# Router of a mixture of experts: rows transposed in place, plain float32 products with rows stationary

## The chip, the cores and the metric

One core of one Trainium2 chip runs the whole program in one launch. The metric is the device time of one execution in microseconds (us). TensorE is called PE here (its weight loads PEld), VectorE DVE, ScalarE ACT, GpSimd POOL, SyncE SP.

## The reference, cut to what matters

The model has two layers; the change touches the router at the head of the last part. 4096 tokens (4 x 1024) of width 256 come out of a windowed attention with a residual and a layer norm, and go through a layer of 8 experts:

```python
x = _layernorm(x + _L1_attn_ref(x, ...), axis=-1)          # ends the stage before
# _L1_ffn_ref
xt = x.reshape(T, H)                                        # T = 4096, H = 256
scores = jax.nn.softmax(xt @ Wr, axis=-1)                   # Wr: 256 x 8, float32
topk_w, topk_idx = jax.lax.top_k(scores, TOP_K)             # 2 of 8 experts
topk_w = topk_w / (topk_w.sum(axis=-1, keepdims=True) + EPS)
# every token's two experts, silu(x Wg) * (x Wu) @ Wd, weighted; plus a shared expert on all tokens
```

## The kernel before, in words

X holds the tokens in SBUF as 32 tiles of 128 rows x 256 columns; four tiles are a chunk, and there are NCH = 8 chunks. The engines run programs of their own, in the order in which the code writes them, and meet by semaphores. Three stages matter:

- **The attention's tail.** The loop over chunks on PE, `step(c, h)`, makes scores, transposes the exponentials (`p_transpose`, L1795) and makes outputs. DVE adds the residual and takes the statistics, POOL makes the inverse deviation, and ACT normalises the chunk in place in X (`normalise_chunk`, L554, semaphore `c_ln`). With chunk 7 this ends the stage.
- **The router**, which starts when `c_ln` says that all 8 chunks are normalised. For each chunk DVE copies the rows to `dxc` (L1354), PE transposes the 8 blocks of 128 x 128 (`x_transpose`, L1857) into PSUM, ACT rounds the result to `DTh` (L608), and DVE takes the rest to `DTl` (L1358), both in the float32r format. PE then makes the logits of 512 tokens with the router's weights stationary (8 columns) and the rows moving (512 columns), as three products of high and low parts for each half of the width (`three`, L1577 to L1579): 6 matmuls. They come out as 8 x 512, by expert; ACT copies them to `lgT` (L618), PE turns them by four small transposes (`by_token`, L1875), and DVE copies them to `lg` (L1362).
- **The routing and what hangs on it.** DVE alone takes the softmax, the two best experts, the counts and each token's place (L1394 to L1468), with one exponential on ACT and two matmuls on PE between. Its last instruction writes `pos` and raises `d_route`. Then POOL scatters the tokens by 64 indirect DMAs (L869), while PE, ACT and DVE work the shared expert for the first four chunks (`shared`). When both are through, the tiles of the experts begin (L1551 and on), then the shared expert for the other four chunks, the gathers and the last layer norm.

PE's `x_transpose(NCH, ...)` and DVE's `copy_rows(NCH + ...)` repeat the transposes of the same chunks for the shared expert, since `DTh` and `DTl` hold two chunks only.

The router's step on PE and the start of the routing on DVE:

```python
            def route(c, h):
                x_transpose(c + 1, 1 - h, 4 - 4 * h)
                router(c, h)
...
            dve.tensor_reduce(rt[0][:], lg[:], AX.X, ALU.max)
            dve.drain()
            dve.tensor_tensor(lg[:], lg[:], each(rt[0][:]), ALU.subtract).then_inc(d_max, 1)
```

Of the kernel before, what the change touches and what calls it, by code (L numbers as in the profile page):

```python
# [4 lines left out]
F32 = mybir.dt.float32  # L5
F32R = mybir.dt.float32r
BF16 = mybir.dt.bfloat16
U32, U16 = mybir.dt.uint32, mybir.dt.uint16
ALU = mybir.AluOpType
# [66 lines left out]
def build(nc, cst, xT, x, wqkvgT, wave_cols, bias_cols, coupling_rows, woutT, bout, wgu_rows, wd_rows, wqk_T, wo_rows, bo, wr, experts, out):  # L76
    ctx = ExitStack()
    with ctx:
        place = {"at": 0, "top": 0}

        def sb(name, shape, dt=F32):
            size = 2 if dt == BF16 else 4
            for s in shape[1:]:
                size *= s
            t = nc.alloc_sbuf_tensor_at(name, shape, dt, offset=base + place["at"])
            place["at"] += (size + 31) // 32 * 32
            place["top"] = max(place["top"], place["at"])
            return t

        def sem(name):  # L90
# [91 lines left out]
        place["at"] = kept + TOP  # L182
        place["at"] += 4 * 2 * 4 * D
        cw = sb("cw", [P, 3, KD, D])
# [22 lines left out]
        wrr = sb("wrr", [P, KD, E])  # L207
        wrh, wrl = sb("wrh", [P, KD, E], F32R), sb("wrl", [P, KD, E], F32R)
        pos = sb("pos", [P, 2, NT], mybir.dt.int32)
# [28 lines left out]
        past = sb("past", [P, NE + 1])  # L238
        lgT = sb("lgT", [E, 2, CH])
        assert place["at"] <= slot_at + 4 * SLOT  # L240
# [10 lines left out]
        rstd4, nmr4 = sb("rstd4", [P, NCH, 4]), sb("nmr4", [P, NCH, 4])  # L251
        d_sum, d_cnt, d_lt, d_lth = sem("d_sum"), sem("d_cnt"), sem("d_lt"), sem("d_lth")
        (d_ld, d_xc, d_xt, d_xhi, d_xlo, d_lg, d_lgc, d_max, d_exp, d_oh, d_pre, d_route, d_sc, d_raw, d_shi, d_slo, d_gu, d_si,
         d_hb, d_hhi, d_hlo, d_dn, d_add, d_xe0, d_xe1, e_t, e_xhi, e_xlo, e_gu, e_si, e_hb, e_ht, e_hhi, e_hlo, e_dn, e_y,
         e_st0, e_st1, w_ready, d_mv, d_rs, d_ln) = (sem("d_" + n) for n in (
            "ld", "xc", "xt", "xhi", "xlo", "lg", "lgc", "max", "exp", "oh", "pre", "route", "sc", "raw", "shi", "slo", "gu", "si",
            "hb", "hhi", "hlo", "dn", "add", "xe0", "xe1", "et", "exhi", "exlo", "egu", "esi", "ehb", "eht", "ehhi", "ehlo",
# [80 lines left out]
        def _(act):  # L338
# [234 lines left out]
            normalise(NP - 1, 1)  # L573

            def step_chunk(c, h):
                if live(c, 0, NCH):
                    exponentials(c, 0)
                if live(c, -2, NCH - 2):
                    x_high(c + 2, h)
                if live(c, 0, NCH):  # L580
                    exponentials(c, 1)
                if live(c, -1, NCH - 1):
                    y_high(c + 1, 1 - h)
                if live(c, 0, NCH):
                    p_high(c)
                if live(c, -1, NCH - 1):
                    z_high(c + 1, 1 - h)
                if live(c, 1, NCH + 1):
                    normalise_chunk(c - 1, 1 - h)
# [8 lines left out]
            act.activation(SWh[:], raw[:, 1], ACT.Copy).then_inc(d_shi, 1)  # L598
            act.wait_ge(d_ld, 16)
            act.activation(wrh[:], wrr[:], ACT.Copy).then_inc(d_shi, 1)  # L600
            for c in range(NCH - 2, NCH + 1):
                step_chunk(c, c % 2)


# [4 lines left out]

            def routed(c, h):  # L610

                wait(act, d_lt, c - 1)
                x_high(c, h, 4 * h)

            def logits(c, h):
                act.wait_ge(d_lt, c + 1)
                wait(act, d_lg, c - 1)
                act.activation(lgT[:, h], PS[0:E, 2 + h], ACT.Copy).then_inc(d_lth, 1)  # L618

            routed(0, 0)  # L620
            routed(1, 1)
            logits(0, 0)
            with act.Fori(1, B) as b:
                for h in range(2):
                    routed(2 * b + h, h)
                    logits(2 * b + h - 1, 1 - h)
            logits(NCH - 1, 1)
            act.wait_ge(d_max, 1)
# [3 lines left out]
            def shared(c, h, after=True):  # L632
# [8 lines left out]
                if after:  # L641
                    x_high(NCH + c + 1, 1 - h, 0)

# [27 lines left out]

            x_high(NCH, 0, 0)
            shared(0, 0)
# [239 lines left out]
        def _(dve):  # L913
# [426 lines left out]
            with dve.Fori(1, B - 1) as b:  # L1340
                for h in range(2):
                    step(2 * b + h, h)
            dve.wait_ge(d_shi, 2)
            dve.tensor_tensor(SWl[:], raw[:, 1], SWh[:].bitcast(F32), ALU.subtract).then_inc(d_slo, 1)
            dve.tensor_tensor(wrl[:], wrr[:], wrh[:].bitcast(F32), ALU.subtract).then_inc(d_slo, 1)
            for c in range(NCH - 2, NCH + 1):
# [12 lines left out]

            def logits(c, h):  # L1360
                dve.wait_ge(d_lg, c + 1)
                dve.tensor_copy(lg[:, bass.ds(4 * c, 4)], PS[:, 6 + h, 0:4 * E].rearrange("p (w e) -> p w e", e=E)).then_inc(d_lgc, 1)  # L1362


            dve.wait_ge(c_ln, NCH)
            copy_rows(0, 0, 0)
            copy_rows(1, 1, 1)
            x_low(0, 0, 0)
            copy_rows(2, 2, 0)
            x_low(1, 1, 4)  # L1370
            with dve.Fori(0, B - 2) as b:
                for h in range(2):
                    c = 2 * b + h
                    copy_rows(c + 3, c + 3, 1 - h)
                    x_low(c + 2, h, 4 * h)
                    logits(c, h)
            copy_rows(NCH - 1, NCH - 1, 1)
            x_low(NCH - 2, 0, 0)
            logits(NCH - 4, 0)
            copy_rows(NCH, 0, 0)  # L1380
            x_low(NCH - 1, 1, 4)
            logits(NCH - 3, 1)
            copy_rows(NCH + 1, 1, 1)
            logits(NCH - 2, 0)
            logits(NCH - 1, 1)
            dve.drain()

# [9 lines left out]

            dve.tensor_reduce(rt[0][:], lg[:], AX.X, ALU.max)
            dve.drain()
            dve.tensor_tensor(lg[:], lg[:], each(rt[0][:]), ALU.subtract).then_inc(d_max, 1)  # L1400
            dve.wait_ge(d_exp, 1)
# [87 lines left out]
            def shared(c, h, early, after=True, done=()):  # L1489
# [8 lines left out]
                if after:  # L1498
                    x_low(NCH + c + 1, 1 - h, 0)
                    if not isinstance(c, int) or c + 2 < NCH:  # L1500
                        copy_rows(NCH + c + 2, c + 2, h)
                for d in done:
# [40 lines left out]

            x_low(NCH, 0, 0)
            shared(0, 0, True)
            shared(1, 1, True)
            with dve.Fori(1, EARLY // 2) as b:
                for h in range(2):
                    shared(2 * b + h, h, True)
            dve.wait_ge(d_shi, 3)  # L1550
            dve.tensor_tensor(EWs[:, EW:SLOT], raw[:, 0], EWs[:, 0:EW].bitcast(F32), ALU.subtract).then_inc(w_ready, 1)  # L1551
# [22 lines left out]
        def _(pe):  # L1574
# [269 lines left out]
            values(0, 0)  # L1844
            for c in range(NCH):
                step(c, c % 2)


            pe.wait_ge(c_res, 4 * NCH)

# [8 lines left out]

            def router(c, h):  # L1860
                pe.wait_ge(d_xlo, c + 1)

                wait(pe, d_lth, c)
                wait(pe, d_lgc, c - 2)
                for k in range(KD):
                    mm = three(PS[0:E, 2 + h], wrh[:, k], wrl[:, k], DTh[:, h, k], DTl[:, h, k], k == 0, k == KD - 1)
                mm.then_inc(d_lt, 1)

            def by_token(c, h):

                if isinstance(c, int) and c == NCH - 1:
                    pe.wait_ge(d_lth, NCH)
                    pe.wait_ge(d_lgc, NCH - 2)
                for w in range(4):
                    t = pe.transpose(PS[:, 6 + h, w * E:(w + 1) * E], lgT[:, h, w * P:(w + 1) * P], ident[0:E, 0:E])  # L1875
                t.then_inc(d_lg, 1)

            def route(c, h):
                x_transpose(c + 1, 1 - h, 4 - 4 * h)
                router(c, h)  # L1880

            pe.wait_ge(d_slo, 2)
            x_transpose(0, 0, 0)
            route(0, 0)
            route(1, 1)
            by_token(0, 0)
            with pe.Fori(1, B - 1) as b:
                for h in range(2):
                    route(2 * b + h, h)
                    by_token(2 * b + h - 1, 1 - h)  # L1890
            route(NCH - 2, 0)
            by_token(NCH - 3, 1)
            router(NCH - 1, 1)
            by_token(NCH - 2, 0)
            by_token(NCH - 1, 1)

            pe.wait_ge(d_oh, 1)
            pe.matmul(PS[:, 4, 0:NT * E], tri[:], ohr[:], start=True, stop=True).then_inc(d_pre, 1)
            pe.matmul(PS[:, 5, 0:NT * E], ones[:], ohr[:], start=True, stop=True).then_inc(d_pre, 1)
            x_transpose(NCH, 0, 0)  # L1900

            def shared(c, h, after=True):
                pe.wait_ge(d_xlo, c + NCH + 1)
                for j in range(4):
# [9 lines left out]
                if after:  # L1914
                    x_transpose(NCH + c + 1, 1 - h, 0)
                for w in range(4):
# [159 lines left out]
```

## Time and profile before

| | |
|---|---|
| median of 3 runs | 1211.71 us (1211.48 to 1213.06) |
| the profiled execution, its own time | 1211.7 us |
| its span, first to last instruction | 1209.9 us |
| PE busy | 1039.7 us (86%) |
| DVE busy | 805.6 us (67%) |
| ACT busy, POOL busy | 467.9 us (39%), 446.5 us (37%) |
| mean granted TensorE clock | 0.939 of full speed |

The profile gives each instruction's start and duration. A matmul's duration holds its latency, so a row of matmuls overlaps and its pace is read from the distance between starts. "Granted clock" is the share of full speed (2.4 GHz) that TensorE was given: 1.00 or 0.50 at any one time, and a mean between them over a stretch.

### The profile page before, as it was taken

What the parts mean: (1) busy time and instruction counts of PE and PEld (TensorE: products, weight loads), DVE (VectorE), ACT (ScalarE), POOL (GpSimd) and SP (SyncE); (2) the same over time, 40 slices, a digit from 0 to 9 for tenths busy, and PEclk for the clock granted to TensorE, in tenths of its full rate; (3) what the DMA queues carried; (4) which work ended last, traced back from release to release, by engine and by line L of the source; (5) the groups of instructions that cost most, each with busy time, mean ns of one, the idle gap of its engine ahead of it and who ended that gap; (6) DMA issues with size and microseconds to landing.
All of it is one profiled execution on the core that took longest, in us unless ns stands there. A gap on an engine that the chain in (4) does not pass through costs nothing.

```text
span 1209.9 us, 19337 instructions
## 1 busy us (share of the span) xinstructions
PE 1039.7 (86%) x5928; PEld 907.7 (75%) x5929; DVE 805.6 (67%) x1361; ACT 467.9 (39%) x799; POOL 446.5 (37%) x357
## 2 busy tenths in 40 slices
PE   4789972589999999998675987999999999998872
PEld 3567741589999998997644876888888888887762
DVE  7978898799999986787566344444444444443775
ACT  6726523244444435565442132332223323322225
POOL 3302003134444456231104777244413431005764
PEclk9989986799999999999787898999999999999896
DMA  6110020900000000200001221333223131112324
GB/s 272 36 35 1 1 78 1 337 3 1 0 0 0 0 2 1 106 1 34 20 1 52 101 101 57 105 104 108 70 86 104 52 108 53 52 48 75 102 81 170
DMA packets 42387, 77.30 MB, mean 64 GB/s; under 512 B 5474, under 2 KB 32868, under 8 KB 40932
## 3 DMA queue, kind: packets, MB, share of 16 engines
q1 hardware_dynamic: 24532, 40.52, 9.3%
q0 software_dynamic: 7008, 26.22, 6.6%
q10 hardware_dynamic: 10800, 9.94, 2.7%
q8 instruction: 28, 0.46, 0.2%
q14 instruction: 19, 0.16, 0.0%
HBM read 45.47 MB, written 31.20 MB: 63 GB/s over the span
## 4 chain that ended last, share of the span: by engine, by line
PE 61%; DVE 13%; issue 9%; DVEq 6%; POOL 6%; ACT 3%; POOLq 1%; DMA 1%; ACTq 0%
PE PS L1577 16%; PE PS L1579 15%; PE PS L1578 15%; POOL gathered L886 5%; PE PS L1701 4%; PE PS L1947 3%; PE PS L1606 2%; DVEq L1101 1%; PE PS L1931 1%; PE PS L1619 1%; DVEq L1206 1%; DVEq L1114 1%; ACT X L703 1%; PE PS L1694 1%; DVEq L1218 1%
## 5 line engine op out<-in xcount | busy, mean ns | idle before, releaser
L1521 DVE TENSOR_TENSOR hb<-PS,gs 128x512 f32<-128x512 f32 x71 | 49.1, 692 | 153.2 <-ACT gs L652 153.2
L1577 PE MATMUL PS<-EWs,xeh 128*128 x284 | 119.2, 420 | 2.2 <-DVE xel L1515 2.2
L1579 PE MATMUL PS<-EWs,xel 128*128 x284 | 112.3, 395 | 0.0
L1578 PE MATMUL PS<-EWs,xeh 128*128 x284 | 111.9, 394 | 0.0
L886 POOL DMA_INDIRECT gathered<-expert_outputs,pos x64 | 63.1, 986 | 115.3 <-DMA expert_outputs<-ye 96.0
L1577 PE MATMUL PS<-WGh,bxh 128*128 128x352 f32 x256 | 87.2, 341 | 20.5 <-DVE hv L1200 14.3
L652 ACT ACTIVATE gs<-PS 128x512 f32<-128x512 f32 x71 | 42.5, 599 | 160.5 <-PE PS L1579 160.5
L860 POOL TENSOR_TENSOR EWs<-raw,zrow 128x3072 fp32r<-128x3072 f32 x7 | 47.7, 6816 | 149.8 <-PE PS L1579 149.7
L1701 PE MATMUL PS<-WD,htf 128*128 128x256 f32 x384 | 88.5, 380 | 1.6 <-ACT htf L470 1.5
L869 POOL DMA_INDIRECT tokens_by_expert<-X,pos x64 | 64.6, 1009 | 67.8 <-DVE pos L1468 48.5
L1577 PE MATMUL PS<-EWs,heh 128*128 x284 | 85.9, 303 | 1.6 <-DVE hel L1525 1.6
L1578 PE MATMUL PS<-WGl,bxh 128*128 128x352 f32 x256 | 84.3, 329 | 0.0
L1579 PE MATMUL PS<-WGh,bxl 128*128 128x352 f32 x256 | 84.3, 329 | 0.0
L1525 DVE TENSOR_TENSOR hel<-PS,heh 128x512 fp32r<-128x512 f32 x71 | 49.1, 692 | 47.8 <-ACT heh L657 47.8
L1578 PE MATMUL PS<-EWs,heh 128*128 x284 | 80.1, 282 | 0.0
L1579 PE MATMUL PS<-EWs,hel 128*128 x284 | 80.1, 282 | 0.0
L1701 PEld LDWEIGHTS PS<-WD,htf 128*128 128x128 f32 x384 | 71.2, 190 | 10.9 <-ACT htf L470 2.5
L657 ACT ACTIVATE heh<-PS 128x512 fp32r<-128x512 f32 x71 | 42.5, 599 | 91.1 <-PE PS L1947 91.1
L1577 PE MATMUL PS<-xh,WQh 128*128 128x512 f32 x128 | 52.8, 413 | 20.8 <-DVE WQl L936 13.4
L1577 PEld LDWEIGHTS PS<-WGh,bxh 128*128 128x128 f32 x256 | 49.6, 194 | 24.3 <-issue 15.5
L1577 PEld LDWEIGHTS PS<-EWs,xeh 128*128 128x128 f32 x284 | 53.7, 189 | 14.5 <-issue 2.4
L1577 PE MATMUL PS<-SWh,Hh 128*128 128x256 f32 x128 | 41.3, 323 | 25.5 <-DVE Hl L1495 25.5
(338 smaller groups left out, 3093.3 us busy)
## 6 DMA issues: line engine op xcount, KB each, us to landing
raw<-experts POOLq DMA_DIRECT2D x6, 1536.0 KB, 7.3
tokens_by_expert<-zrow SPq DMA_DIRECT2D x1, 9088.0 KB, 29.3
xe<-tokens_by_expert ACTq DMA_DIRECT2D x71, 128.0 KB, 2.0
expert_outputs<-ye SPq DMA_DIRECT2D x71, 128.0 KB, 1.7
raw<-experts SPq DMA_DIRECT2D x3, 1536.0 KB, 6.3
xraw<-xT SPq DMA_DIRECT2D x8, 512.0 KB, 5.6
X<-x SPq DMA_DIRECT2D x1, 4096.0 KB, 16.8
y<-X SPq DMA_DIRECT2D x8, 512.0 KB, 2.6
```

What stands on the lines that cost most here:

```text
L652: act.activation(gs[:, h], PS[:, 2], ACT.Silu).then_inc(e_si, 1)
L657: act.activation(heh[:, h].rearrange("p a c -> p (a c)"), PS[:, 4 + h], ACT.Copy).then_inc(e_hhi, 1)
L860: pool.tensor_tensor(hi, src, zrow[:, :].unsqueeze(1).to_broadcast([P, EW // D, D]), ALU.add)
L869: pool.indirect_dma_start(out=XS, out_offset=bass.IndirectOffsetOnAxis(ap=pos[:, j, t:t + 1], axis=0), in_=X[:, t], in_offset=None).then_i ...
L886: pool.indirect_dma_start(out=gathered[c][:, j, t], out_offset=None, in_=YS, in_offset=bass.IndirectOffsetOnAxis(ap=pos[:, j, 4 * c + t:4 ...
L1521: dve.tensor_tensor(hb[:, h], PS[:, 3], gs[:, h], ALU.mult).then_inc(e_hb, 1)
L1525: dve.tensor_tensor(hel[:, h].rearrange("p a c -> p (a c)"), PS[:, 4 + h], heh[:, h].rearrange("p a c -> p (a c)").bitcast(F32), ALU.subtr ...
L1577: pe.matmul(out_, wh, vh, start=first, stop=False)
L1578: pe.matmul(out_, wh, vl, start=False, stop=False)
L1579: return pe.matmul(out_, wl, vh, start=False, stop=last_)
L1701: mm = pe.matmul(PS[:, 7, i * D:(i + 1) * D], htf[:, i, k], WD[:, k], start=k == 0, stop=k == FT - 1)
L1947: t = pe.transpose(PS[:, 4 + h, j * P:(j + 1) * P], hb[:, h, j * P:(j + 1) * P], ident)
```

## The change

The router no longer shares the path of the shared expert. PE transposes the rows straight from X, each chunk as soon as it is normalised; those of chunks 0 and 1 stand inside the attention's last step. ACT copies each result whole to `rx` (float32, two chunks). The logits of 128 tokens are then two plain float32 products with the rows stationary (128 x 128) and the router's weights moving (8 columns), which come out by token; those of all 8 chunks lie side by side in one bank of PSUM, from which DVE's first reduction reads. The copies to `dxc` for the router, the high and low parts of rows and router weights, the copies to `lgT` and `lg` and the small transposes go away. On ACT, the copies of chunks 0 and 1 stand before the normalisation of chunk 6, those of chunks 2, 3 and 4 before that of chunk 7, the others behind it. On DVE the two copies for the shared expert and the casts of `tri` and `ones` come ahead of the wait for the logits. The diff, cut to its core (what is left out renames semaphores and counts, and shifts the shared expert's chunk numbers by NCH):

```diff
@@ scalar
+            def rows_copied(c):
+                act.wait_ge(d_rt, c + 1)
+                wait(act, d_lg, c - 1)
+                bank = c % 2 * 4
+                act.activation(rx[:, c % 2], PS[:, bank:bank + 2], ACT.Copy).then_inc(d_rx, 1)
@@ scalar, step_chunk: before normalise_chunk(c - 1, 1 - h)
+                if isinstance(c, int) and c == NCH - 1:
+                    rows_copied(0)
+                    rows_copied(1)
+                if isinstance(c, int) and c == NCH:
+                    for n in range(2, 5):
+                        rows_copied(n)
                 if live(c, 1, NCH + 1):
                     normalise_chunk(c - 1, 1 - h)
...
-            act.wait_ge(d_ld, 16)
-            act.activation(wrh[:], wrr[:], ACT.Copy).then_inc(d_shi, 1)
             for c in range(NCH - 2, NCH + 1):
                 step_chunk(c, c % 2)
+            for c in range(5, NCH):
+                rows_copied(c)
...
-            routed(0, 0)
-            routed(1, 1)
-            logits(0, 0)
-            with act.Fori(1, B) as b:
-                for h in range(2):
-                    routed(2 * b + h, h)
-                    logits(2 * b + h - 1, 1 - h)
-            logits(NCH - 1, 1)
@@ vector
-            dve.tensor_tensor(wrl[:], wrr[:], wrh[:].bitcast(F32), ALU.subtract).then_inc(d_slo, 1)
...
-            dve.wait_ge(c_ln, NCH)
+            dve.wait_ge(c_ln, 2)
             copy_rows(0, 0, 0)
             copy_rows(1, 1, 1)
-            x_low(0, 0, 0)
...
-            logits(NCH - 1, 1)
-            dve.drain()
...
-            dve.tensor_reduce(rt[0][:], lg[:], AX.X, ALU.max)
+            dve.wait_ge(d_lg, NCH)
+            logits = PS[:, 6, 0:NT * E].rearrange("p (t e) -> p t e", e=E)
+            dve.tensor_reduce(rt[0][:], logits, AX.X, ALU.max)
             dve.drain()
-            dve.tensor_tensor(lg[:], lg[:], each(rt[0][:]), ALU.subtract).then_inc(d_max, 1)
+            dve.tensor_tensor(lg[:], logits, each(rt[0][:]), ALU.subtract).then_inc(d_max, 1)
@@ tensor
-            for c in range(NCH):
-                step(c, c % 2)
-            pe.wait_ge(c_res, 4 * NCH)
+            for c in range(NCH - 1):
+                step(c, c % 2)
+
+            def rows_transposed(c):
+                pe.wait_ge(c_ln, c + 1)
+                wait(pe, d_rx, c - 1)
+                bank = c % 2 * 4
+                for k in range(KD):
+                    for w in range(4):
+                        t = pe.transpose(PS[:, bank + k, w * P:(w + 1) * P], X[:, 4 * c + w, k * P:(k + 1) * P], ident)
+                t.then_inc(d_rt, 1)
+
+            def logits(c):
+                pe.wait_ge(d_rx, c + 1)
+                for w in range(4):
+                    for k in range(KD):
+                        at = (4 * c + w) * E
+                        mm = pe.matmul(PS[:, 6, at:at + E], rx[:, c % 2, k, w * P:(w + 1) * P], wrr[:, k], start=k == 0, stop=k == KD - 1)
+                mm.then_inc(d_lg, 1)
+
+            scores(NCH - 1, 1)
+            pe.wait_ge(c_zlo, NCH + NCH // 2)
+            rows_transposed(0)
+            p_transpose(NCH - 1)
+            pe.wait_ge(c_max, 2 * NCH)
+            rows_transposed(1)
+            outputs(NCH - 1, 1)
+            pe.wait_ge(d_ld, 16)
+            for c in range(NCH):
+                logits(c)
+                if c + 2 < NCH:
+                    rows_transposed(c + 2)
...
-            route(0, 0)
-            route(1, 1)
-            by_token(0, 0)
...
-            by_token(NCH - 1, 1)
```

## Rows read from the trace of the kernel before

**Rows 1.** The page: the chain that ended last, share of the span by engine.

```profile
PE 61%; DVE 13%; issue 9%; DVEq 6%; POOL 6%; ACT 3%; POOLq 1%; DMA 1%; ACTq 0%
```

**Rows 2.** The chain that ended last: start us, us, engine, tile and line.

```profile
600.30 2.08 ACT X L554 x4
...
603.24 1.96 PE PS L1857 x8
...
630.52 0.43 DVE lg L1400
...
647.83 1.14 DVE DTl L1358
...
734.83 3.35 DVE EWs L1551
```

**Rows 3.** Stretches: length; busy (count) of PE, PEld, DVE, ACT, POOL; PEclk, DMA share, GB/s.

```profile
586.90:590.90 4.00, 1.75 (x8) 0.83 (x9) 3.85 (x14) 3.27 (x10) 0.56 (x3) 0.99 0.00 0
590.90:594.10 3.20, 3.19 (x15) 3.20 (x16) 0.62 (x2) 2.02 (x4) 1.00 (x2) 0.50 0.00 0
...
595.50:603.20 7.70, 0.00 (x0) 0.00 (x0) 3.46 (x12) 2.07 (x4) 1.56 (x4) 0.64 0.00 1
603.20:606.90 3.70, 3.65 (x16) 3.28 (x16) 1.12 (x2) 1.02 (x1) 0.00 (x0) 0.50 0.00 0
...
607.70:629.50 21.80, 20.46 (x128) 11.51 (x126) 14.14 (x23) 11.12 (x15) 0.00 (x0) 1.00 0.00 1
```

**Rows 4.** Timeline of one chunk of the router: start us, us, engine, line.

```profile
612.11 1.09 PE L1857 MATMUL PS<-C,dxc 128*128 128x128 f32 x8
...
612.96 0.48 PE L1577 MATMUL PS<-DTh,wrh 128*8 128x512 f32 x1
...
613.24 1.03 ACT L608 ACTIVATE DTh<-PS 128x1024 fp32r<-128x1024 f32 x1 [0.70 <-PE PS L1857]
...
614.53 0.41 PE L1875 MATMUL PS<-C,lgT 8*128 8x8 f32 x4
...
614.87 1.09 PE L1857 MATMUL PS<-C,dxc 128*128 128x128 f32 x8
...
630.03 0.42 DVE L1398 TENSOR_REDUCE rt<-lg 128x32 f32<-128x256 f32 x1
```

**Rows 5.** Timeline of the attention's last step on PE and ACT.

```profile
587.67 0.93 PE L1795 MATMUL PS<-C,sc 128*128 128x128 f32 x4 [0.81 <-ACT sc L543]
589.05 0.93 PE L1795 MATMUL PS<-C,sc 128*128 128x128 f32 x4 [0.44 <-ACT sc L543]
590.91 0.55 PE L1577 MATMUL PS<-Zh,PTh 128*128 128x256 f32 x1 [0.93 <-DVE PTl L1299]
...
595.19 0.28 PE L1579 MATMUL PS<-Zh,PTl 128*128 128x256 f32 x1
...
589.39 1.22 ACT L549 ACTIVATE PTh<-PS 128x512 fp32r<-128x512 f32 x2
```

**Rows 6.** Loads and matmuls: timeline, then two lines' minimum/median/maximum ns.

```profile
591.47 0.41 PE L1579 MATMUL PS<-Zh,PTl 128*128 128x256 f32 x1
591.68 0.41 PE L1577 MATMUL PS<-Zh,PTh 128*128 128x256 f32 x1
...
594.37 0.28 PE L1578 MATMUL PS<-Zl,PTh 128*128 128x256 f32 x1
...
594.49 0.28 PE L1579 MATMUL PS<-Zh,PTl 128*128 128x256 f32 x1
...
402.93 2.76 PE L1701 MATMUL PS<-WD,htf 128*128 128x256 f32 x12
...
L1701 PEld LDWEIGHTS PS<-WD,htf x384: 186/190/192, 261.0 to 482.6; 128*128 128x128 f32 x192
L1701 PE MATMUL PS<-WD,htf x384: 377/379/483, 261.2 to 482.9; 128*128 128x256 f32 x192
...
L1875 PE MATMUL PS<-C,lgT x32: 200/202/224, 611.8 to 629.1; 8*128 8x8 f32 x32
```

More of the change, by code:

```diff
@@ L182, in build @@
         place["at"] = kept + TOP
-        place["at"] += 4 * 2 * 4 * D
+        rx = sb("rx", [P, 2, KD, CH])
         cw = sb("cw", [P, 3, KD, D])
@@ L207, in build @@
         wrr = sb("wrr", [P, KD, E])
-        wrh, wrl = sb("wrh", [P, KD, E], F32R), sb("wrl", [P, KD, E], F32R)
         pos = sb("pos", [P, 2, NT], mybir.dt.int32)
@@ L238, in build @@
         past = sb("past", [P, NE + 1])
-        lgT = sb("lgT", [E, 2, CH])
         assert place["at"] <= slot_at + 4 * SLOT
@@ L251, in build @@
         rstd4, nmr4 = sb("rstd4", [P, NCH, 4]), sb("nmr4", [P, NCH, 4])
-        d_sum, d_cnt, d_lt, d_lth = sem("d_sum"), sem("d_cnt"), sem("d_lt"), sem("d_lth")
-        (d_ld, d_xc, d_xt, d_xhi, d_xlo, d_lg, d_lgc, d_max, d_exp, d_oh, d_pre, d_route, d_sc, d_raw, d_shi, d_slo, d_gu, d_si,
+        d_sum, d_cnt, d_rt, d_rx = sem("d_sum"), sem("d_cnt"), sem("d_rt"), sem("d_rx")
+        (d_ld, d_xc, d_xt, d_xhi, d_xlo, d_lg, d_max, d_exp, d_oh, d_pre, d_route, d_sc, d_raw, d_shi, d_slo, d_gu, d_si,
          d_hb, d_hhi, d_hlo, d_dn, d_add, d_xe0, d_xe1, e_t, e_xhi, e_xlo, e_gu, e_si, e_hb, e_ht, e_hhi, e_hlo, e_dn, e_y,
          e_st0, e_st1, w_ready, d_mv, d_rs, d_ln) = (sem("d_" + n) for n in (
-            "ld", "xc", "xt", "xhi", "xlo", "lg", "lgc", "max", "exp", "oh", "pre", "route", "sc", "raw", "shi", "slo", "gu", "si",
+            "ld", "xc", "xt", "xhi", "xlo", "lg", "max", "exp", "oh", "pre", "route", "sc", "raw", "shi", "slo", "gu", "si",
             "hb", "hhi", "hlo", "dn", "add", "xe0", "xe1", "et", "exhi", "exlo", "egu", "esi", "ehb", "eht", "ehhi", "ehlo",
@@ L608, in x_high @@
                 act.activation(DTh[:, h], PS[:, bank:bank + 2], ACT.Copy).then_inc(d_xhi, 1)
[L610 to L618, printed above, removed]
-            routed(0, 0)
-            routed(1, 1)
-            logits(0, 0)
-            with act.Fori(1, B) as b:
-                for h in range(2):
-                    routed(2 * b + h, h)
-                    logits(2 * b + h - 1, 1 - h)
-            logits(NCH - 1, 1)
             act.wait_ge(d_max, 1)
@@ L641, in shared @@
                 if after:
-                    x_high(NCH + c + 1, 1 - h, 0)
+                    x_high(c + 1, 1 - h, 0)
             def x_high_e(i, h):
@@ L670, in tile @@
                         rows(i + 3, 1 - h)
-            x_high(NCH, 0, 0)
+            x_high(0, 0, 0)
             shared(0, 0)
@@ L1342, in _ @@
                     step(2 * b + h, h)
-            dve.wait_ge(d_shi, 2)
+            dve.wait_ge(d_shi, 1)
             dve.tensor_tensor(SWl[:], raw[:, 1], SWh[:].bitcast(F32), ALU.subtract).then_inc(d_slo, 1)
-            dve.tensor_tensor(wrl[:], wrr[:], wrh[:].bitcast(F32), ALU.subtract).then_inc(d_slo, 1)
             for c in range(NCH - 2, NCH + 1):
@@ L1358, in x_low @@
                 dve.tensor_tensor(DTl[:, h], PS[:, bank:bank + 2], DTh[:, h].bitcast(F32), ALU.subtract).then_inc(d_xlo, 1)
-            def logits(c, h):
-                dve.wait_ge(d_lg, c + 1)
-                dve.tensor_copy(lg[:, bass.ds(4 * c, 4)], PS[:, 6 + h, 0:4 * E].rearrange("p (w e) -> p w e", e=E)).then_inc(d_lgc, 1)
-            dve.wait_ge(c_ln, NCH)
+            dve.wait_ge(c_ln, 2)
             copy_rows(0, 0, 0)
             copy_rows(1, 1, 1)
-            x_low(0, 0, 0)
[L1369 to L1384, printed above, removed]
-            logits(NCH - 1, 1)
-            dve.drain()
             def each(v):
@@ L1498, in shared @@
                 if after:
-                    x_low(NCH + c + 1, 1 - h, 0)
+                    x_low(c + 1, 1 - h, 0)
                     if not isinstance(c, int) or c + 2 < NCH:
-                        copy_rows(NCH + c + 2, c + 2, h)
+                        copy_rows(c + 2, c + 2, h)
                 for d in done:
@@ L1542, in tile @@
                     y_out(i - 1, 1 - h)
-            x_low(NCH, 0, 0)
+            x_low(0, 0, 0)
             shared(0, 0, True)
@@ L1549, in _ @@
                     shared(2 * b + h, h, True)
-            dve.wait_ge(d_shi, 3)
+            dve.wait_ge(d_shi, 2)
             dve.tensor_tensor(EWs[:, EW:SLOT], raw[:, 0], EWs[:, 0:EW].bitcast(F32), ALU.subtract).then_inc(w_ready, 1)
@@ L1858, in x_transpose @@
                 t.then_inc(d_xt, 1)
[L1860 to L1883, printed above, removed]
-            route(0, 0)
-            route(1, 1)
-            by_token(0, 0)
[L1887 to L1894, printed above, removed]
-            by_token(NCH - 1, 1)
+            pe.wait_ge(d_slo, 1)
             pe.wait_ge(d_oh, 1)
@@ L1899, in _ @@
             pe.matmul(PS[:, 5, 0:NT * E], ones[:], ohr[:], start=True, stop=True).then_inc(d_pre, 1)
-            x_transpose(NCH, 0, 0)
+            x_transpose(0, 0, 0)
             def shared(c, h, after=True):
-                pe.wait_ge(d_xlo, c + NCH + 1)
+                pe.wait_ge(d_xlo, c + 1)
                 for j in range(4):
@@ L1914, in shared @@
                 if after:
-                    x_transpose(NCH + c + 1, 1 - h, 0)
+                    x_transpose(c + 1, 1 - h, 0)
                 for w in range(4):
```

## The prediction

> **What bounds the kernel now.** I read the page first: PE is busy 86% of the span (the table above) and stands for 61% of the chain, DVE for 13% [rows 1]. So the whole is PE's, but the router has to be read by itself. The chain in order of time shows there what sets the end: ACT's last normalisation from 600.30, the router from 603.24 with PE's transposes at the head of each chunk, then DVE alone (the subtraction of L1400 at 630.52) until the routing is out and it takes up `DTl` for the shared expert at 647.83; from there 87.0 us to L1551 at 734.83, with which the experts begin [rows 2]. The stage is a line of engines waiting for one another before and after the router, so an earlier end of the router moves all that follows by the same amount. The stretches then say how full PE was: it did nothing from 595.5 to 603.2, in the 7.7 us between the last attention matmul and the router's first transposes, and was busy 20.46 of 21.80 us from 607.7 to 629.5 [rows 3]. The timeline gives one chunk: transposes at 612.11, the next ones at 614.87, that is 2.76 us a chunk; and DVE's first reduction starts at 630.03 [rows 4]. That start is what I forecast.
>
> **What does not move.** From the first reduction on, the same instructions run in the same order. The 64 scatters on POOL and the shared expert both start from `pos`, and no transfer that they need is late: in the stretches that cover the router the DMA engines are all but idle [rows 3], so the zero fill of the scatter's target and the expert's weights have landed. The saving at the reduction should reach the end whole.
>
> **The floor.** Chunk 7 is normalised at 602.38 [rows 2]. Its transposes (0.9), ACT's copy (1.03, as L608 [rows 4]) and its logits (1.9, below) put the reduction at 606.4 at the earliest. It would save 23.6 us. The forecast asks what PE's work adds to that.
>
> **When PE is free.** Before, outputs of chunk 7 start at 590.91, when DVE's `PTl` is there, and end near 595.4 [rows 5]; most of them run at the half clock (0.50 from 590.9 to 594.1), after a stretch of 4.00 us in which PE was busy 1.75 [rows 3]. The change puts 8 transposes before `p_transpose` and 8 behind it. Eight take 0.86 us: they start at 612.11 and the next group at 612.96 [rows 4]. The first set runs from about 586.8, where PE waited for ACT until 587.67; the second from 589.6, where it waited for DVE until 590.91 [rows 5]. Both are covered by those waits; uncovered they would cost 0.9 each. ACT's copies of chunks 0 and 1 (2.1 us) come behind `PTh`, which is done at 590.61 [rows 5], so the outputs don't wait for them; they push the normalisation of chunk 6 by about 0.5 us, which only the transposes of chunk 6 need, much later. With PE busier I take the full clock for the outputs: 24 matmuls at 0.12 are 2.8 us, free at 593.8. If they are as slow as before, it is 1.6 us later.
>
> **What is removed.** Per chunk six matmuls of 512 moving columns, four small transposes, the DVE copy and subtraction, ACT's `lgT`: together with the 8 transposes the 2.76 us. The chain lay over PE, ACT and DVE in turn. The high and low parts of the router's weights go from ACT and DVE too, inside the attention, where neither is the last wait; I count nothing.
>
> **What a float32 product costs.** A plain float32 product is two loads and two matmuls: L1701 has 384 records for 32 x 6 = 192 products [rows 6]. The logits of a chunk are 8 products, 16 pairs, each with a load of 128 columns and a matmul of 8. No row has this pair. From below: the small transposes, 8 moving columns and 128 loaded ones in one pass, follow each other at (0.41 - 0.20)/3 = 0.07 us [rows 4, 6]. From above: L1701 with 256 moving columns goes at (2.76 - 0.38)/11 = 0.216 [rows 6]. Between them lie the pairs of the outputs, with loads of 128 columns too: seven steps from 594.37 to 595.19, 0.117 each [rows 5, 6]. A load of that size therefore needs no more than 0.117, and with only 8 columns moving I expect it alone to set the pace. I take 0.117: 1.87 us a chunk. The ends are 1.1 and 3.5.
>
> The Trainium skill ("TensorE: Matmul & The Clock Gate", LDWEIGHTS) gives a load its columns over 1.2 in ns, 107 ns for 128. By that the 128 pairs would take 1.3 us less than by the rows; an estimate, and no row shows a load by itself.
>
> **Who is last in the new loop.** PE: 1.87 + 0.86 = 2.73 a chunk. ACT: one copy of 1.03, and it comes back while PE does a chunk's logits and the next transposes, so no logits wait. Rows copied 2 to 4 stand ahead of the normalisation of chunk 7 on ACT: copy 4 is done near 603.5, so chunk 7 is normalised near 605.5 in place of 602.38. The POOL step waits for nothing of it, and its transposes come only near 610. Hidden, with 4 us to spare.
>
> **The sum at the full clock.** Eight logits 15.0, six sets of transposes 5.2, and 14 starts of a group behind a semaphore at 0.08 (the small transposes end issuing near 614.80, the next group starts at 614.87 [rows 4]) 1.1: 21.3 us from 593.8 gives 615.1. The end of the last matmul and DVE's start add 0.3: the reduction at 615.4 in place of 630.03 [rows 4]. DVE's own work ahead (two copies, two casts, 2 us) is long done. Saved 14.6 us. The profiled execution took 1211.7 (its span and 1.8 around it), the same as the median: 1197.1.
>
> **The clock.** The new loop asks little of the array: of 2.73 us, matmuls of 8 columns fill the larger part. The rows: PE empty from 595.5 on, the clock fell; a mean of 0.64 over 7.7 us is 2.2 us at full and 5.5 at half, so it fell near 597.7. Sixteen transposes from 603.2, PE busy 3.65 of 3.70 us, ran at 0.50, and the clock was back at 1.00 from 607.7 [rows 3]. With the 8 transposes from 587.67 alone, busy 1.75 of 4.00, it fell too. So PE's busy share matters, and transposes count. What the rows don't show is whether loads with 8-column matmuls count as work. The skill's same page (PE-mode transpose) says that transposes don't engage the full clock as matmuls do; the trace disagrees, since after 16 transposes and hardly anything else the clock rose. By the page the new loop would hold nothing that keeps the clock, and the time would be that of rival 1.
>
> **Rival 1: the clock halves in the loop.** At half clock the pair is 0.21 (591.47 to 591.68 [rows 6]) and eight transposes 1.8 (3.65 for sixteen [rows 3]): 5.3 a chunk with its gaps in place of 2.9, 1.8 times. If it falls near 597.7 as before, 3.9 of the 21.3 us are done and 17.4 become 31.3: the reduction at 629.3, 0.7 saved, 1211.0. A fall 3 us later gives 1208.6; one from the start of the loop 1214.1. It wouldn't recover before the routing. For it: PE's array is empty for most of the loop, and 1.75 of 4.00 busy wasn't enough. Against it: PE is never idle, its weight path is full, and transposes, which move few columns too, brought the clock back.
>
> **Rival 2, slower: load and matmul in series.** If an 8-column matmul is too short to cover the next load, a pair costs its two records, 0.19 for the load and 0.20 for a matmul of 8 columns (L1875), 0.39 at the full clock [rows 6]: 6.2 a chunk, 50 for eight, the reduction at 650.3, 1232.0. It decides from 0.23 a pair: there the saving is gone. For it: no row has a full float32 load with so short a matmul. Against it: the small transposes follow each other at 0.07, though one lasts 0.20 [rows 6].
>
> **Rival 3: the pair at one of its ends.** At 0.07 the loop takes 9.0 + 5.2 + 1.1 = 15.3, the reduction at 609.4, 20.6 saved: 1191.1. At 0.216 it takes 33.9, the reduction at 628.0, 2.0 saved: 1209.7.
>
> **Rival 4: the transposes delay the attention's tail.** If PE reaches `p_transpose` late by both sets, 1.7 us go to the outputs and to the start of the loop: 1198.8. It can't turn the sign.
>
> **How the numbers follow.** Forecast (full clock) 0.45, own range 1194 to 1200 (the outputs' clock 1.6, the pair between 0.10 and 0.13). Rival 1 0.33. Rival 2 0.07. Rival 3 0.06 at each end, rival 4 0.03. A change under 0.2%, 2.4 us, can't be told from none. Faster: the forecast, the cheap pair, half of the dear one, rival 4 and a quarter of rival 1, 0.65. Slower: rival 2 and a fifth of rival 1, 0.14. The rest 0.21. The range goes from 1192, toward the cheap pair, to 1214, which takes in rival 1; left out are rival 2 and the cheapest pair.
>
> **What would show it.** In the changed profile: the logits' matmuls at 0.117 from start to start; transposes from X inside the attention's last step and `p_transpose` no later than 587.8; PE's outputs ended near 593.8; PE without idle time until 615; granted clock 1.00 from 594 to 615; DVE's reduction near 615.4 and `pos` 17.6 us later. A granted clock of 0.50 in that stretch is rival 1; a start to start over 0.2 at the full clock is rival 2 or 3. Logits that wait for `rx` would mean that ACT, not PE, is last, which the sum excludes.

## The result, and the profile after

| | before | after |
|---|---|---|
| median of 8 runs | 1212.87 us (1211.37 to 1215.99) | 1209.46 us (1207.26 to 1211.82) |
| the profiled execution, its span | 1211.7, 1209.9 us | 1211.1, 1209.3 us |
| mean granted TensorE clock of the profiled execution | 0.939 | 0.928 |

The ratio is 0.9968, 95% interval 0.9954 to 0.9981: 3.9 us faster by the ratio (3.4 by the difference of the medians), where 14.6 were forecast. The kernel got faster, the range (1192 to 1214) holds the time, and the size is a quarter of the forecast one. It is nearest to what rival 1 gave (0.7 to 3.1 us).

The two profiled executions differ by only 0.6 us, because the stages ahead of the router took 3.9 us longer in the second (what lies behind the reduction took 1.1 us less). These stages are all but the same code; PE's clock changes at other moments in them from one execution to the next (from 200 to 250 us it was 0.78 in the first and 0.67 in the second). So I count from the last matmul of the attention's last scores, which ends at 586.87 in the profile before (start 586.59 and 0.28) and at 590.74 in the one after. From there to DVE's first reduction the kernel before takes 43.2 us (to 630.03 [rows 4]) and the changed one 39.8. That is 3.4 us less, as much as the medians differ by.

PE's timeline of the changed kernel in the attention's last step (start us, us; the answer to [rows 5]):

```profile
590.46 0.28 PE L1548 MATMUL PS<-XTh,YTl 128*128 128x256 f32 x1
590.58 1.04 PE L1823 MATMUL PS<-C,X 128*128 128x128 f32 x8
...
591.55 0.93 PE L1764 MATMUL PS<-C,sc 128*128 128x128 f32 x4
...
593.69 1.04 PE L1823 MATMUL PS<-C,X 128*128 128x128 f32 x8
...
594.78 0.35 PE L1546 MATMUL PS<-Zh,PTh 128*128 128x256 f32 x1
```

L1823 is the transposes from X. The first set stands where PE waited before, and `p_transpose` (L1764) starts 0.81 us after the scores' end; before it was 0.80. The second ends as the outputs start. The outputs start 4.04 us after the scores' end, as before, and are through at 597.82: 3.0 us, not the 4.6 of before.

The loop of the router, from its first logits (L1831) to the reduction (the answer to [rows 4]):

```profile
597.66 1.84 PE L1831 MATMUL PS<-wrr,rx 128*128 128x8 f32 x16
599.36 1.07 PE L1823 MATMUL PS<-C,X 128*128 128x128 f32 x8
600.27 1.85 PE L1831 MATMUL PS<-wrr,rx 128*128 128x8 f32 x16
...
601.97 1.81 PE L1823 MATMUL PS<-C,X 128*128 128x128 f32 x8
...
603.58 3.42 PE L1831 MATMUL PS<-wrr,rx 128*128 128x8 f32 x16
...
606.86 1.95 PE L1823 MATMUL PS<-C,X 128*128 128x128 f32 x8
608.60 3.42 PE L1831 MATMUL PS<-wrr,rx 128*128 128x8 f32 x16
...
630.51 0.42 DVE L1367 TENSOR_REDUCE rt<-PS 128x32 f32<-128x256 f32 x1 [28.36 <-PE PS L1831]
```

Read the distance between the starts of L1831. The first two groups are 2.61 us apart; 603.58 and 608.60 are 5.02 apart. Sixteen pairs took 1.70 us (597.66 to 599.36), then 3.28 (603.58 to 606.86). The stretches (columns as in [rows 3]) say why:

```profile
594.80:597.50 2.70, 2.70 (x23) 2.70 (x24) 1.31 (x3) 2.70 (x5) 0.97 (x2) 1.00 0.00 0
597.50:602.10 4.60, 4.60 (x44) 4.60 (x43) 4.06 (x14) 1.79 (x3) 1.18 (x3) 1.00 0.00 2
602.10:630.40 28.30, 28.30 (x137) 28.27 (x135) 0.05 (x1) 7.08 (x9) 1.18 (x2) 0.50 0.00 1
```

The granted clock is 1.00 for the first 4.3 us of the loop and 0.50 from 602.1 to its end. PE is busy for all of these 28.30 us, its weight path for 28.27, and ACT for 7.08, so nobody but PE sets the pace.

### The profile page after: what moved, and what is told of

It reads as the page before. It is cut to its first block, busy times and chain, and to the rows that moved or that the text cites. A ratio compares the mean times of both kernels' runs of the same rounds, so it can differ in the third digit from the quotient of the medians.

```text
span 1209.3 us, 19343 instructions
## 1 busy us (share of the span) xinstructions
PE 1052.5 (87%) x5976; PEld 927.6 (77%) x5977; DVE 790.2 (65%) x1336; ACT 462.7 (38%) x790; POOL 444.3 (37%) x357
## 4 chain that ended last, share of the span: by engine, by line
PE 54%; DVE 13%; POOL 11%; DVEq 9%; issue 8%; ACT 3%; DMA 1%; POOLq 1%; ACTq 0%
PE PS L1546 14%; PE PS L1548 13%; PE PS L1547 13%; POOL tokens_by_expert L861 5%; POOL gathered L878 5%; PE PS L1907 3%; PE PS L1670 2%; DVEq L1093 2%; PE PS L1831 2%; DVEq L1198 2%; PE PS L1575 2%; PE PS L1891 1%; DVE hx L1105 1%; PE PS L1588 1%; DVEq L1210 1%
## 5 line engine op out<-in xcount | busy, mean ns | idle before, releaser
L1546 PE MATMUL PS<-WGh,bxh 128*128 128x352 f32 x256 | 88.4, 345 | 19.9 <-DVE hv L1192 13.6
L1548 PEld LDWEIGHTS PS<-EWs,xel 128*128 128x128 f32 x284 | 53.7, 189 | 10.7
```

Of the source, the lines that this page charges most:

```text
L1546: pe.matmul(out_, wh, vh, start=first, stop=False)
L1548: return pe.matmul(out_, wl, vh, start=False, stop=last_)
```

## The experiments

Theory A: the clock halves because little moves through the array while loads of 128 columns and matmuls of 8 take turns, and what is missing from the forecast is that alone. Theory B: the loop is slow for what it loads and reads, and the width of the moving operand doesn't matter. Theory C: an earlier reduction is given back further on.

The runs of the experiments form three groups, each on a chip of its own, and in all of them every kernel took some 118 to 120 us more, the one before too (medians 1330.66, 1333.23 and 1330.77 us). The extra time lies behind the router: in the stretch 648 to 735, PE was busy 32.56 of 87.00 us in the repeated changed kernel (after_again), against 77.46 in the kernel before in its first profile. There it stands again and again for 2.2 to 2.4 us between two matmuls of the shared expert without a wait that the trace shows (the page's chain calls this "issue": 15% of the chain in after_again, 8% in the changed kernel's first profile). Why is open. The router's stage of the changed kernel has the same length to within 0.4 us (39.8 and 40.2), and each ratio is to the kernel before in the same group. The kernel before was profiled only once, on the first chip, so the 43.2 us are from there. "To the reduction" is always from the end of the attention's last scores, in the one profiled execution of each run.

| run | edit | to the reduction, us | clock in the loop | ratio to before, 95% interval |
|---|---|---|---|---|
| (before) | | 43.2 | 0.50, then 1.00 | 1 |
| after_again | the changed kernel | 40.2 | 1.00, then 0.50 | 0.9972 (0.9949 to 0.9995) |
| wide8 | 64 columns move | 26.3 | 1.00 | 0.9875 (0.9843 to 0.9906) |
| wide8_again | the same | 26.3 | 1.00 | 0.9890 (0.9866 to 0.9914) |
| wide4 | 32 columns | 26.3 | 1.00 | one run: 1316.62 us, before 1333.23 |
| wide4_timed | the same | 26.3 | 1.00 | 0.9877 (0.9853 to 0.9900) |
| wide2 | 16 columns | 39.8 | 1.00, then 0.50 | one run: 1336.16 us, before 1333.23 |
| filler | 8, and other matmuls between | 33.0 | 1.00 | 0.9945 (0.9922 to 0.9968) |
| late | first transposes behind the outputs | 44.4 | 1.00, then 0.50 | 0.9993 (0.9968 to 1.0017) |
| early_undone | all behind chunk 7 | 56.8 | 0.50 | 1.010 (1.007 to 1.013) |
| early_undone_wide16 | the same, 128 columns | 40.2 | 0.50, then 1.00 | 0.9978 (0.9953 to 1.0003) |

**The control.** The changed kernel as it is.

> The changed kernel once more, as the control of this call: 0.997 of the kernel before. From the end of the attention's last scores to DVE's first reduction 39.8 us, as in its first profile; the granted clock falls to 0.50 a few us after the attention's last matmul, and from there the pairs of the logits go at 0.21 us in place of 0.117.

Two rows give the length, here and in the runs below: the attention's last matmul of scores and DVE's first reduction.

```profile
586.75 0.28 PE L1548 MATMUL PS<-XTh,YTl 128*128 128x256 f32 x1
...
627.21 0.42 DVE L1367 TENSOR_REDUCE rt<-PS 128x32 f32<-128x256 f32 x1 [28.77 <-PE PS L1831]
```

Its reduction came 40.2 us after the scores, the clock fell 3.9 us after the outputs, and the ratio repeats the first.

**More columns, same result.** The weights are read several times over; the next product overwrites the surplus.

```diff
-mm = pe.matmul(PS[:, 6, at:at + E], rx[:, c % 2, k, w * P:(w + 1) * P], wrr[:, k], start=k == 0, stop=k == KD - 1)
+mm = pe.matmul(PS[:, 6, at:at + 8 * E].rearrange("p (r e) -> p r e", e=E), rx[:, c % 2, k, w * P:(w + 1) * P],
+               wrr[:, k].unsqueeze(1).to_broadcast([P, 8, E]), start=k == 0, stop=k == KD - 1)
```

> The router's weights are read eight times over as the moving operand, 64 columns in place of 8; the next product writes over the surplus, so the logits are the same. Theory A (the clock: too few columns move, and the clock halves): 64 float32 columns in two passes hide behind the load, so the pair stays at 0.117 us, the granted clock stays at 1.00, the reduction comes 28.5 us after the end of the scores, and the time is 0.988 of before (14.5 us less). Theory B (the loop is slow for what it loads and reads, whatever moves): nothing changes against the changed kernel, 0.997. Theory C (the gain at the reduction is given back further on): the reduction at 28.5 us, but the time stays at 0.997.

PE's timeline and one stretch of the loop of wide8:

```profile
586.76 0.28 PE L1548 MATMUL PS<-XTh,YTl 128*128 128x256 f32 x1
...
593.96 1.89 PE L1831 MATMUL PS<-wrr,rx 128*128 128x64 f32 x16
595.68 1.04 PE L1823 MATMUL PS<-C,X 128*128 128x128 f32 x8
596.57 1.90 PE L1831 MATMUL PS<-wrr,rx 128*128 128x64 f32 x16
...
593.90:613.20 19.30, 19.30 (x178) 19.28 (x177) 4.11 (x14) 8.65 (x12) 2.36 (x4) 1.00 0.00 1
...
613.35 0.42 DVE L1367 TENSOR_REDUCE rt<-PS 128x32 f32<-128x256 f32 x1 [14.91 <-PE PS L1831]
```

Eight times the moving columns, and a chunk takes 2.61 us to the end of the loop in place of 5.02. The clock is 1.00 for all of it. Theory B falls; so does C, since 16.9 us less to the reduction came out as 16.6 us in the time (0.9875 of 1330.66), and as 14.6 (0.9890 of 1330.77) in the last group. Theory A said 28.5 to the reduction; it is 26.3. The pair costs 0.107 us and not 0.117 (593.96 to 595.68, 16 pairs), which is 1.2 of the 2.2 us; most of the rest is the 0.08 us that the sum had for each start of a group, and which hardly shows: eight transposes take 0.89 us with both of their starts (595.68 to 596.57).

> The version with 64 moving columns once more, as the best so far, timed in another call: reduction 26.3 us after the end of the scores, 16.8 us earlier than in the kernel before; about 0.987 of before, by theory A. Theory C would have it at 0.997.

**Fewer of them.** The same edit with 4 and 2 in place of 8.

> The changed kernel with 32 moving columns. Theory A: if this is enough, the clock stays and the reduction comes 26.3 us after the end of the scores as with 64 columns; if not, between that and 40. Theory B: 40 us.

> The version with 32 moving columns, timed. Theory A: the load sets the pace with 32 columns as with 64, so both take the same time, 0.987 of before. If in some executions 32 columns are too few to keep the clock, its median lies above that of 64 columns.

> The changed kernel with 16 moving columns in place of 8. Theory A: still few columns move beside the load; the clock may fall a little later than with 8, reduction 33 to 40 us after the end of the scores. Theory B: 40 us.

With 32 columns the two profiled executions look as with 64, and so does the time. With 16 the loop of wide2 goes like that with 8: 39.8 us, which is the upper end of theory A's range and theory B's 40 too, so this run doesn't tell the two apart. Its two stretches:

```profile
597.30:601.80 4.50, 4.50 (x44) 4.50 (x43) 4.11 (x14) 1.63 (x3) 1.24 (x3) 1.00 0.01 2
601.80:630.10 28.30, 28.30 (x136) 28.19 (x134) 0.00 (x0) 7.08 (x9) 1.12 (x2) 0.50 0.00 1
```

**The width left alone.** The wide runs changed the logits' matmuls themselves. Here these stay at 8 columns, and two products that nobody reads stand in each chunk, so what changes is the clock and the surplus work alone.

```diff
                         mm = pe.matmul(PS[:, 6, at:at + E], rx[...], wrr[:, k], ...)
+                    if w % 2:
+                        pe.matmul(PS[:, 7, 0:D], ident, X[:, 4 * c + w], start=True, stop=True)
                 mm.then_inc(d_lg, 1)
```

> The logits stay at 8 moving columns; behind every second group of them stands one float32 product of the identity with 256 columns of X into an unused bank, 2 in a chunk, 0.43 us each at the full clock, 6.8 us in all. Theory A: the clock stays at 1.00, the reduction comes 35 us after the end of the scores, 0.993 of before. Theory B: 13.7 us of work at the half clock on top of the changed kernel, reduction at 53 us, 1.008.

The timeline of filler, and its loop as one stretch:

```profile
588.59 0.28 PE L1548 MATMUL PS<-XTh,YTl 128*128 128x256 f32 x1
...
598.43 1.04 PE L1823 MATMUL PS<-C,X 128*128 128x128 f32 x8
599.31 0.96 PE L1831 MATMUL PS<-wrr,rx 128*128 128x8 f32 x8
600.12 0.68 PE L1833 MATMUL PS<-X,C 128*128 128x256 f32 x2
...
595.70:622.00 26.30, 26.30 (x210) 25.23 (x209) 4.21 (x15) 8.78 (x12) 2.36 (x4) 1.00 0.01 2
...
621.90 0.42 DVE L1367 TENSOR_REDUCE rt<-PS 128x32 f32<-128x256 f32 x1 [21.63 <-PE PS L1831]
```

A kernel with more work on the busiest engine is faster than the one without: 33.0 us to the reduction in place of 40.2, and the logits have 8 columns still. The surplus costs 6.7 us (33.0 less the 26.3 of wide8) and buys back 13.9 (40.2 less 26.3). Theory A had 35 us, too late by the same two terms as above. By the ratio it is 7.3 us faster than the kernel before (interval 4.3 to 10.4), where the reduction of the profiled execution is 10.1 earlier.

**The transposes in the attention's tail.** Chunks 0 and 1 are transposed behind the outputs.

```diff
-            rows_transposed(0)
             p_transpose(NCH - 1)
             pe.wait_ge(c_max, 2 * NCH)
-            rows_transposed(1)
             outputs(NCH - 1, 1)
             pe.wait_ge(d_ld, 16)
+            rows_transposed(0)
+            rows_transposed(1)
```

> The transposes of chunks 0 and 1 move from the attention's last step to behind its outputs; ACT's copies of them then come after that too, before the normalisation of chunk 6. Both theories: PE has 1.7 to 3.4 us more to do after the outputs. If the transposes had kept the clock up for the outputs, these run at 0.50 again (1.6 us). The reduction at 42 to 45 us after the end of the scores, 0.999 to 1.001 of before.

The outputs of late, and its loop:

```profile
590.50:595.10 4.60, 4.54 (x25) 4.57 (x26) 1.39 (x3) 0.00 (x0) 1.05 (x2) 0.63 0.00 0
597.10:600.80 3.70, 3.66 (x34) 3.66 (x34) 2.30 (x10) 3.60 (x6) 2.36 (x4) 1.00 0.01 2
600.90:630.80 29.90, 29.90 (x144) 29.84 (x143) 0.00 (x0) 7.25 (x10) 0.00 (x0) 0.50 0.00 1
```

Its scores end at 586.52 and its reduction starts at 630.87. Without the 16 transposes in PE's waits the outputs take 4.6 us again, most of them at the half clock, as before [rows 3]. With them they take 3.0. So the transposes filled idle time and kept the clock as well; together 4.2 us to the reduction, against the changed kernel in the same group.

**The early start undone.** All transposes and copies for the router wait for chunk 7, as the router did before; the products stay.

```diff
@@ scalar, step_chunk
-                if isinstance(c, int) and c == NCH - 1:
-                    rows_copied(0)
-                    rows_copied(1)
-                if isinstance(c, int) and c == NCH:
-                    for n in range(2, 5):
-                        rows_copied(n)
...
-            for c in range(5, NCH):
+            for c in range(NCH):
                 rows_copied(c)
@@ tensor
-            rows_transposed(0)
             p_transpose(NCH - 1)
             pe.wait_ge(c_max, 2 * NCH)
-            rows_transposed(1)
             outputs(NCH - 1, 1)
             pe.wait_ge(d_ld, 16)
+            pe.wait_ge(c_ln, NCH)
+            rows_transposed(0)
+            rows_transposed(1)
```

> The early start alone undone: all transposes from X, and all copies to rx, come behind the normalisation of chunk 7, as the router did before; products of 8 columns as in the changed kernel. Theory A: the loop starts at the half clock 16 us after the end of the scores and stays there: 8 x 5.0 us and the first sets, so the reduction comes 56 to 58 us after the end of the scores, 14 us later than in the kernel before: 1.011 of before. Theory B, in which the products themselves are cheaper than before and only the late start was paid: the reduction at 16 + 24 = 40 us, 0.997.

> The same with the weights read sixteen times over, 128 moving columns. Theory A: the clock comes back to 1.00 some us into the loop and stays; two chunks at 5.0 us and six at 2.6 and the first sets, reduction 42 to 46 us after the end of the scores, within 0.3% of before. Theory B: as early_undone or slower.

First early_undone (rows and two stretches), then early_undone_wide16:

```profile
589.71 0.28 PE L1542 MATMUL PS<-XTh,YTl 128*128 128x256 f32 x1
...
606.41 3.65 PE L1817 MATMUL PS<-C,X 128*128 128x128 f32 x16 [7.80 <-issue]
609.85 3.42 PE L1825 MATMUL PS<-wrr,rx 128*128 128x8 f32 x16
...
646.80 0.42 DVE L1361 TENSOR_REDUCE rt<-PS 128x32 f32<-128x256 f32 x1 [43.86 <-PE PS L1825]
...
606.40:609.80 3.40, 3.39 (x16) 3.40 (x17) 0.00 (x0) 1.02 (x1) 0.00 (x0) 0.50 0.00 0
609.80:646.70 36.90, 36.90 (x178) 36.87 (x176) 0.00 (x0) 7.17 (x7) 0.00 (x0) 0.50 0.00 0
```

```profile
586.46 0.28 PE L1542 MATMUL PS<-XTh,YTl 128*128 128x256 f32 x1
...
603.18 3.65 PE L1817 MATMUL PS<-C,X 128*128 128x128 f32 x16 [7.81 <-issue]
606.62 2.58 PE L1825 MATMUL PS<-wrr,rx 128*128 128x128 f32 x16
...
626.98 0.42 DVE L1361 TENSOR_REDUCE rt<-PS 128x32 f32<-128x256 f32 x1 [27.28 <-PE PS L1825]
...
603.10:607.90 4.80, 4.72 (x22) 4.75 (x23) 0.00 (x0) 2.05 (x2) 0.00 (x0) 0.50 0.00 0
607.90:626.90 19.00, 19.00 (x171) 18.85 (x170) 0.00 (x0) 6.14 (x6) 0.00 (x0) 1.00 0.00 1
```

This takes the change apart. With the new products and the old start the reduction comes 13.6 us later than in the kernel before (56.81 against 43.16): the loop of 8 columns at the half clock costs that. The early start brings it 17.0 us forward (to 39.77; against the 40.2 of after_again it is 16.6). The change is the difference, 3.4. With 128 columns and the late start the clock comes back 4.7 us into the work and stays, 40.2 us in all; there the early start is worth 13.9 more (26.3). Theory A had 42 to 46 us for that run, since it put two whole chunks at the half clock, and the clock came back within the first.

The sixteen transposes at the head of early_undone also answer a reading of the prediction, that transposes brought the clock back in the kernel before. There 16 of them ran at 0.50 from 603.24, PE then waited 0.67 us, and the clock rose at 607.9, 0.3 us into the first matmul of 512 columns. Here 16 of them ran at 0.50 from 606.41, pairs of 8 columns followed, and the clock didn't rise in 40 us. With 128 columns behind the same transposes it rose 4.7 us after their start. So the runs don't show that transposes alone bring the clock back: it rose where wide matmuls followed them, and not where pairs of 8 columns did, in one profiled execution each.

## Why the prediction was right and where it failed

**The step that failed** is the one headed "The clock", and with it "The sum at the full clock", which the forecast took as the likeliest case (0.45 against 0.33 for rival 1). It gave as the reason that PE is never idle, that its weight path is full, and that transposes had brought the clock back. PE was never idle and its weight path was full, 28.27 of 28.30 us, and the clock halved all the same. At 0.50 a chunk took 5.02 us, where the sum has 2.89 with its two starts. With PE just as busy, the clock stayed when 32 or 64 columns moved in place of 8, or when other matmuls stood between. The runs show this dependence; what exactly the chip counts stays open. Rival 1 had the mechanism and nearly the size: 39.8 us to the reduction, where its first case has 42.4, and 3.9 us saved, where it put 0.7, and 3.1 for a later fall. Its chunk at the half clock was 5.3 us and measured 5.02, which over six chunks is most of the difference. It had the fall 3.9 us after the outputs, and it came at 4.3, but that is luck in part: it took the moment of the kernel before, where PE had gone idle at 595.5.

**What a float32 product costs** was read well enough from its neighbours, and slightly too dear: 0.107 us in place of 0.117 at the full clock, 0.205 in place of 0.21 at the half. The page of the Trainium skill that the prediction weighed ("TensorE: Matmul & The Clock Gate", LDWEIGHTS), columns over 1.2 in ns, gives 107 ns, and the trace agrees at the full clock; at the half clock a pair took 0.205 us. Load and matmul overlap at 8 columns too, so rivals 2 and 3 are out. The 14 starts of a group, 1.1 us in the sum, came to some 0.2.

**When PE is free** was right: outputs at the full clock, 3.0 us for 2.8, and `p_transpose` not later than before. Rival 4 didn't happen. The run named late shows that it was the transposes in PE's waits that held the clock there.

**Who is last in the loop** was right: no group of L1831 or L1823 has idle time ahead of it. ACT normalises chunk 7 only from 609.76 to 611.82, and its transposes come 10 us after that. In wide8, at the full clock, it is done at 604.97 and its transposes start at 608.75, which is the slack of 4 us that the forecast gave.

**What does not move** was right. From the reduction to the cast that writes `pos` it is 17.6 us before and after (630.03 to 647.63, 630.51 to 648.13), and the runs with 64 columns carry their 16.9 us through to within the interval, though on their chips the stages behind took longer.

**The size of the full-clock case** was nearly right, on a kernel that has it: 14.6 us were forecast, and the reduction comes 16.9 earlier with 32 or 64 columns (14.6 to 16.6 by the ratios). The terms of the sum were 2.2 us too dear, as said above.

The version to keep is the changed kernel with 32 or 64 moving columns: 0.988 of the kernel before and about 0.991 of the changed one.

## What to carry to other kernels

A product turned so that its moving side is narrow can be right in every duration and still slow the engine for itself and its neighbours: take the granted clock as a quantity of its own, and don't conclude from a full busy share that it holds. Where loads of weights set the pace, moving more columns costs little: at the full clock a pair took 0.106 us with 8, 16 or 32 columns, about 0.108 with 64 and 0.112 with 128. So widening the moving operand is a cheap thing to try. And when a change both starts something earlier and changes what it does, undo the start alone: here one was worth 17.0 us and the other cost 13.6, and the sum of 3.4 hid both.

## What the runs showed of the hardware

- TensorE can be at its lower level (1.2 GHz) while the profile shows it busy without a gap: 28.3 us at 0.50 after 4.3 us of the same loop at 1.00. The Trainium skill ("TensorE: Matmul & The Clock Gate", Why this matters for your kernels) advises to keep TensorE busy and to leave no idle gaps; in this loop there were none. It didn't come back by itself there, nor in the 36.90 us of early_undone.
- Transposes can hold the clock. Sixteen of them in PE's waits kept it at 1.00 through the outputs in each of eight profiled executions (after, after_again, wide8, wide8_again, wide4, wide4_timed, wide2, filler), and without them it was 0.63 to 0.64 over the outputs in four (the kernel before, late and the two with the early start undone). The Trainium skill ("TensorE: Matmul & The Clock Gate", Part 4: PE-mode transpose) says that the full clock doesn't engage for transposes, which don't count as a busy PE in the same way; the clock over the outputs here disagrees with it. Transposes with pairs of 8 columns between them didn't hold the clock in the loop, nor raise it in early_undone.
